# The order of four partition quarters in the loads of a graph kernel's adjacency matrix: 0, 1, 2, 3 in place of 0, 2, 1, 3

## What is computed

```python
h = jnp.maximum(_layernorm(x), 0.0)
d = 1.0 / jnp.sqrt(jnp.sum(adj, axis=-1))
z = leaky_relu((d[:, None] * (adj @ (d[:, None] * h))) @ W1 + b1, 0.1)
S = exp(-sqrt(max(|z_i|^2 + |z_j|^2 - 2 z_i.z_j, 0) + 1e-10) / 2)   # the 4 nearest of a row kept
A2 = S + adj
x = x + lap_mul(A2, h) @ W2 + b2          # lap_mul: degrees of A2 on both sides
h = jnp.maximum(_layernorm(x), 0.0)
x = x + h @ W_self.T + (adj @ h) @ W_neigh.T + b
```

## Time and profile before

| | |
|---|---|
| three timed executions, us | 1172.3, 1177.01, 1194.65; median 1177.01 |
| the profiled execution, us | 1180.82 |
| its span, first to last instruction, us | 1178.8 |
| granted TensorE clock, mean over the span | 0.917 |
| busy shares of the span | PE 79%, DVE 74%, POOL 58%, ACT 48% |
| bytes moved by DMA | 369.10 MB, mean 313 GB/s |
| transfers of line 389 | 704, from 3.8 to 474.2 us of the span |

### The profile page before, as it was taken

How to read it: one execution, slowest core, us unless ns; L and a number is a source line. 1 busy time by engine, 2 the same in 40 slices (tenths; PEclk the granted TensorE clock), 3 DMA queues, 4 the chain that set the end, 5 groups by cost and what they waited for, 6 DMA issues and landing times.

```text
span 1178.8 us, 12596 instructions
## 1 busy us (share of the span) xinstructions
PE 929.5 (79%) x3378; PEld 583.5 (50%) x3378; DVE 868.9 (74%) x960; ACT 566.7 (48%) x1171; POOL 680.8 (58%) x1103
## 2 busy tenths in 40 slices
PE   0146437549559788769999999979989997999997
PEld 0023213224224333346766766435656645788886
DVE  2648558757768999747999998627687648888884
ACT  2454434545422221147777778424334433676763
POOL 9999988878673668104555565667777763000000
PEclk9987679689789888979999999999999998899999
DMA  9999999999999999739766767998989997699992
GB/s 210 293 315 321 330 331 363 341 335 359 361 333 358 339 313 356 296 125 367 260 250 247 256 235 270 395 412 316 349 299 356 371 341 269 248 369 383 376 387 90
DMA packets 98750, 369.10 MB, mean 313 GB/s; under 512 B 21264, under 2 KB 34320, under 8 KB 73872
## 3 DMA queue, kind: packets, MB, share of 16 engines
q1 hardware_dynamic: 51696, 258.43, 56.6%
q0 software_dynamic: 40960, 103.87, 30.7%
q10 hardware_dynamic: 6048, 6.29, 1.6%
HBM read 244.78 MB, written 123.73 MB: 313 GB/s over the span
## 4 chain that ended last, share of the span: by engine, by line
PE 41%; DVE 7%; POOL 5%; issue 4%; DMA 3%; ACT 2%; POOLq 0%; ACTq 0%; DVEq 0%
PE ps L1362 6%; PE ps L1380 5%; PE ps L1381 5%; PE ps L1382 5%; PE ps L1363 5%; PE ps L1364 5%; PE ps L1389 4%; POOL zt_lo L613 3%; PE ps L1359 2%; DVE araw_r L1207 2%; DVE araw L936 1%; DMA araw<-in_adj_dram 1%; DVE out_t L1164 1%; PE ps L1259 1%; PE ps L1271 1%
## 5 line engine op out<-in xcount | busy, mean ns | idle before, releaser
L389 POOL DMA_DIRECT2D araw<-in_adj_dram x704 | 382.7, 552 | 88.5 <-DVE tr L936 48.9
L1207 DVE TENSOR_TENSOR araw_r<-araw,tr_r 128x512 fp32r<-128x512 f32 (+1 forms) x184 | 213.9, 1220 | 63.4 <-ACT tr_r L815 63.3
L815 ACT ACTIVATE tr_r<-araw 128x2048 fp32r<-128x2048 f32 x88 | 166.3, 1910 | 74.4 <-DMA araw<-transposed 29.6
L613 POOL DMA_INDIRECT zt_lo<-neighbour_table,idx_st x128 | 144.2, 1126 | 48.8 <-issue 42.3
L761 ACT ACTIVATE araw<-ps,nsq 128x1024 f32<-128x1024 f32 x128 | 142.6, 1117 | 55.4 <-PE ps L1364 55.4
L1271 PE MATMUL ps<-tr,ys 128*128 128x512 f32 x256 | 130.7, 661 | 35.5 <-DVE ys L943 28.5
L659 ACT ACTIVATE ps<-araw 128x256 f32<-128x256 f32 x304 | 111.6, 367 | 81.9 <-DMA araw<-in_adj_dram 81.4
L936 DVE STREAM_TRANSPOSE tr<-araw 128x2048 f32<-128x2048 f32 x32 | 123.3, 3873 | 30.3 <-DMA araw<-in_adj_dram 26.7
L1389 PE MATMUL ps<-araw,ys 128*128 128x512 f32 x320 | 142.9, 602 | 2.6 <-ACT ys L806 2.6
L1362 PE MATMUL ps<-zt_lo,zs_hi 128*128 128x512 f32 x256 | 108.8, 425 | 0.0
L1066 DVE TENSOR_REDUCE bmax<-araw 128x64 f32<-128x4096 f32 x23 | 101.5, 4411 | 9.4 <-ACT araw L761 7.4
(11 more groups left out here) (164 smaller groups left out, 1460.7 us busy)
## 6 DMA issues: line engine op xcount, KB each, us to landing
araw<-transposed SPq DMA_DIRECT2D x128, 1024.0 KB, 7.1
araw<-in_adj_dram POOLq DMA_DIRECT2D x704, 128.0 KB, 16.2
keys_scratch<-araw SPq DMA_DIRECT2D x96, 512.0 KB, 3.5
transposed<-tr SPq DMA_DIRECT2D x32, 1024.0 KB, 8.6
transposed<-unit_zt_hi SPq DMA_DIRECT2D x8, 1024.0 KB, 9.3
transposed<-unit_zt_lo SPq DMA_DIRECT2D x8, 1024.0 KB, 8.7
transposed<-unit_sq_rows SPq DMA_DIRECT2D x8, 1024.0 KB, 9.5
transposed<-araw SPq DMA_DIRECT2D x8, 1024.0 KB, 5.3
```

The lines of the kernel that those rows point to most:

```text
L389: gp.dma_start(araw[R * q:R * q + R, place, U * v:U * v + U], adj_v[q, :, g // 2, g % 2, v, :, c]).then_inc(a_first_in[place], DMA)
L613: gp.indirect_dma_start(out=gath[:, i, u, k, :], out_offset=None, in_=table, in_offset=bass.IndirectOffsetOnAxis(ap=idx_st[:, i, u * TOPK ...
L815: act.activation(ring_hi[:, place % TSLOTS], ring[:, j], ACT.Copy).then_inc(hi_done, 1)
L1207: ins = v.tensor_tensor(ring_lo[:, j, u], ring[:, j, u], ring_hi[:, place % TSLOTS, u].bitcast(F32), ALU.subtract)
```

## The change

The inner loop over the quarters, which ran in the order 0, 2, 1, 3, runs in the order 0, 1, 2, 3. So the first transfers of a chunk write the partitions 0 to 31, 32 to 63, 64 to 95, 96 to 127, where they wrote 0 to 31, 64 to 95, 32 to 63, 96 to 127. The same 16 transfers with the same bytes go to the same places of `araw` and count up the same semaphore. The other side changes its order too: the 1 KiB pieces of one matrix row that the four transfers read lie side by side in DRAM, and they are now read in the order in which they lie.

```diff
         def load_chunk(gp, g, c, place):
             for v in range(QD):
-                for q in (0, 2, 1, 3):
+                for q in range(QD):
                     gp.dma_start(araw[R * q:R * q + R, place, U * v:U * v + U],
                                  adj_v[q, :, g // 2, g % 2, v, :, c]).then_inc(a_first_in[place], DMA)
```

## The result

The changed kernel takes 1204.89 us in the median of 5 runs (1197.59 to 1215.58), the kernel before 1177.01 us (1172.3 to 1194.65). The ratio is 1.0287, with a 95% interval of 1.0221 to 1.0353: slower by more than 2%, and inside the range of 1174 to 1221, 7 us above the forecast of 1198. Executions of one kernel come in a faster and a slower state, and every ratio in this document compares those in the faster one alone, so it can differ from the quotient of the medians, which is 1.0237 here. The profiled execution took 1202.32 us with a span of 1200.4, against 1180.82 and 1178.8 before, so 21.5 us or 1.8% more; the forecast for that pair was 1201.9.

A forecast was written before the change was run, and what follows sets the result against it. The first pass was taken as bound by DMA from 20 to 360 us, then by DVE with DMA close behind. 17.2 + 1.9 + 2 = 21.1 us gave 1201.9 profiled, 1198.1 for the median; range 1174 to 1221.

The forecast's parts named there:

- 17.2: First pass, 60 to 360 us, loads without stores beside them: 17.2 us of added time.
- 1.9: Start of the first pass, 20 to 47 us, beside small loads of x: 7% more, 1.9 us.
- two things in which the loads differ from the stores: First-pass loads write 32 partitions at a time and read short runs of 1 KiB.
- half rate: Loads reaching half of the ways into SBUF: 215 GB/s, half of 430, so 610 ns for a transfer.
- 13.3%: Loads without stores beside them: a transfer takes 546 ns, 64 ns or 13.3% more, so 240 GB/s.
- 129.5 us: Time from 60 to 360 us in slices under 300 GB/s, to which the slowdown was applied.
- 3.9: First-pass chunks after 360 us: 3.9 us of DMA work added in 29 us of slices under 300 GB/s.
- Two us: First-pass chunks after 360 us: 2 us of delay, as DVE covers a part of the added DMA work.
- No change: First-pass loads: reads set the rate, so quarter order matters little; 1177 us, at most a few more; chance 0.30.
- Slower by more: First-pass loads, also beside stores: DMA engines out of step collide, 16.7% more time, 42 us, 1219 us; chance 0.25.
- write theory: First-pass loads: neighbouring transfers writing the same half of the ways into SBUF lose the 128 ns a change saves.
- Faster: First-pass loads: reads gain from the order of pieces in DRAM, up to 48 us, 1129 us; chance 0.04.

The follow-up runs named there:

- runs of eight: Loop over quarters outside, row blocks inside, so eight transfers in a row write one half, against the kernel before: 1244.75 us, ratio 1.0503.
- SP's loads alone: Stretches of two runs splitting loads over POOL and SP, against the kernel before: quarters 2, 3 on SP, ratio 1.0316; quarters 1, 3 on SP, 0.9944.
- runs of four: Quarters outside in the order 0, 2, 1, 3, so four transfers in a row write one half, against the kernel before: 1228.73 us, ratio 1.0392.
- the three that go in pairs: Against the kernel before: the changed kernel, 1204.89 us; its write order with the old read order, 1202.48 us; order 0, 3, 2, 1, 1215.05 us.
- writes and reads alone: Two runs against the kernel before: new write order with old read order, 1202.48 us; old write order with new read order, 1183.86 us.
- reads alone: Partitions written in the old order, column pieces read in the new order 0, 1, 2, 3, against the kernel before: 1183.86 us, ratio 1.004.

## Why the prediction was right

**The bound.** Part A was bound by DMA, and what was added to the DMA engines' work came out at its end one for one: 17.2 + 1.9 = 19.1 us were forecast for it, and 20.1 us more work of q0 moved its end by 20.2. In the runs of eight it was 50.1 and 50.4.

**The mechanism.** Writes to one half, not reads: shown by the two halves of the change run apart, and by SP's loads alone, 193 GB/s on one half and 266 on both. The runs of four and eight fit it and reach a plateau at half of the rate beside stores. The split of the partitions into 0 to 63 and 64 to 127, which the forecast assumed, is the only one into two pairs of quarters that fits the orders tried: all that alternate between them come out at 0.98 to 1.01 of the kernel before, the three that go in pairs at 1.02 to 1.03, longer runs at 1.04 and 1.05. The DMA work of q0 over the whole span orders them the same way: 354 to 373 us for the five executions that alternate in both parts besides the kernel before's 362, 380 to 385 for the three in pairs, 410 for runs of four and 425 for runs of eight. The rate of a single stretch orders them less well (247 to 285 GB/s against 234 to 256). In the Trainium skill (SBUF — State Buffer, "Door 1: The DMA port swizzle") 32 partitions reach 8 of the 16 ports; the 205 GB/s of the runs of eight agree with half of the 410 to 430 of the mixed slices. The rule of the Trainium skill that would have made the order worth almost nothing (SBUF — State Buffer, "Can I just issue two DMAs to hit both halves?", a gain of 6%) does not hold for this queue of transfers behind each other: alternating brought 278 against 205 GB/s, 36%.

The prediction names two things in which the loads differ from the stores, and there is a third: loads write SBUF and stores read it. The later passes show that this isn't what makes loads slow. They load units of 128 partitions (L442), and from 1100 to 1110 us before, with nothing beside them:

```profile
q1 hardware_dynamic: 565, 4.11, 99.9%
```

That is 411 GB/s. So even the alternating order, at 278, leaves a third of the rate unused. Whether the 32 partitions or the runs of 1 KiB cost it wasn't tested.

**The sizes.** That the sum came out so well is partly luck. The half rate was taken as 215 GB/s from the mixed slices; the runs of eight show 205. In the 15 us compared above a load alone got slower by 19% and not 13.3%. But over all slices under 300 GB/s from 60 us to the end of part A the mean fell only from 271 to 247, that is 10% more time for the same bytes, and there were 164 us of them in place of 129.5 (31 + 55 + 40 + 38 in the slices after). How much counts as alone hangs on the length of a slice: with at most 1 us throughout it is 141.6 us at 271 before and 171.3 at 246 after. By these, the bytes that ran alone before take 14.4 us longer, where the forecast had 17.2. The start ends at 49 us in place of 47, as forecast with 1.9. The other 4 of the 20.2 us aren't placed by this. They can lie in slices that loads and stores share in part, for which the prediction had taken nothing. The DMA work of q0 grew by 23.4 us, where 17.2 + 1.9 + 3.9 = 23.0 were forecast.

**Part B.** Two us were forecast, 0.6 came by the milestones (20.8 - 20.2), and 4.4 in the run that changed part B alone. That VectorE covers the rest is therefore not shown.

**The chances.** The measured ratio is clear of 2%, where 0.56 stood on within 2% and only 0.41 on slower: the class that came was not the one held likeliest. The forecast of 21.1 us (1.8%) lay close to that line. Between the medians lie 27.9 us, while the two profiled executions differ by 21.5. The other 6 us have no term in the profiles; the executions of the changed kernel alone scatter by 18 us (1197.6 to 1215.6).

**The rivals.** No change fell with the runs of the writes and reads alone. Slower by more, with collisions beside stores as well, fell with the mixed slices, which kept their rate (the slices of 300 GB/s and more from 60 us to the end of part A have a mean of 390 GB/s after and 389 before, and in the runs of eight they still reach 426). Its forecast for loads alone, 16.7% more time or 233 GB/s, was no worse than that of the write theory: 234 was measured in the stretch of 15 us. What lets the same kernel run its loads at 285 GB/s in one execution and 247 in another was not tested; a step between neighbouring engines is one possibility, the chip another. Faster, by the order in DRAM, fell with the reads alone.

## What to carry to other kernels

When loads cover only a part of the partitions, look where in SBUF those next to each other in the queue land, and let them alternate between partitions 0 to 63 and 64 to 127; the order costs nothing, and here it was worth 2 to 3% of the whole kernel. The sign to look for is in the DMA view by slices: engines at a full share with two levels of rate. It doesn't prove the cause, since the reads alone could have given it too; two runs that change the order of the writes and of the reads apart do. Transfers over all 128 partitions ran at 411 GB/s here, against 278 for the alternating quarters; whether this layout could be loaded so was not tried. Splitting such loads over two queues, with one half in each, made this kernel 3% slower; with both halves in each it changed it by half a per cent.

## What the runs showed that was not expected

The same 32-partition transfer goes out from POOL's queue in packets of some 2.7 KB in the mean and from SP's in packets of 0.9 KB, and the queues share an engine by packets, so POOL's get three times the bytes. The mean of POOL's packets has many small ones in it: in the stretch of 85 to 100 us 431 of 1287 are under 512 B, and the other 856 carry the 3.51 MB, 4.1 KB each.

And one kernel can load at different rates from one execution to the next: the order 0, 3, 1, 2 showed 285 and 247 GB/s, and ran between 1157.65 and 1204.1 us on one chip. Up to 46 us the two profiles are alike (223 to 277 GB/s); they part behind that. What decides it stays open.
